# A value stage of graph attention: targets' places broadcast and compared with the lane, in place of one-hots turned on TensorE

## The chip, the core and the metric

The program runs on one core of a Trainium2 chip. Its engines work side by side and meet at semaphores: PE (TensorE: matmuls, and turning tiles by a matmul with the identity), DVE (VectorE), ACT (ScalarE), POOL (GpSimd) and SP, which here issues transfers. The metric is the device time of one execution in microseconds, the median of the runs. Time before: 7192.23 us (three runs, 7168.37 to 7201.24).

## The reference, cut to what matters

Four graph layers follow each other on one graph of 3125 nodes and 53125 edges (sorted by target). The change lies in the second, graph attention with eight heads of 32 features:

```python
def _mhsa(h, edge_bias, src, dst, Wq, Wk, Wv, Wp, bp):
    Q, K, V = h @ Wq, h @ Wk, h @ Wv                 # 3125 x 8 x 32
    score = einsum('ehd,ehd->eh', K[src], Q[dst]) / sqrt(HD) + edge_bias
    m = segment_max(score, dst)
    ex = exp(score - m[dst])
    denom = segment_sum(ex, dst)
    attn = ex / denom[dst]
    out = segment_sum(attn[:, :, None] * V[src], dst)
    return out.reshape(n, DIM) @ Wp + bp
```

The fourth layer needs for each edge one number more, the norm: 1 over the count of edges with the same target and the same of eight types. The kernel takes it from the table of nodes in the same place in which it takes `m[dst]`.

## The kernel before

Edges are sorted by target into 440 tiles of 128 edges; a tile belongs to one of 25 blocks of 128 nodes. Four tiles (U = 4) are a group, so there are 110 groups. Within its block an edge's target has a place from 0 to 127 (column `D_LOC` of `edge_d`). `g.lane` holds each partition's own number.

The score stage (`score_pass`, line 1669 on) computes the scores of all edges, per block and head an upper bound `m`, and the counts per type. Its SP queue stores the gathered V rows sorted by edge in `v_sorted`. Its DVE queue begins with tables, the last of them `type_hot` (L1857), on which PE waits before its loop.

The value stage (`value_pass`) runs over the 110 groups, one instruction stream for each engine; `unrolled(groups, stages)` writes it out, and each stage's number is its lead: at step k a stage with lead 3 works on group k + 3. A queue is in order, so what stands first in the list of stages waits first. Per group n:

- SP loads 512 KB of V rows into one of `VR` = 5 buffers, when `total` has freed it (L1963).
- ACT, `mask`: one-hots of the targets' places, edges on partitions, in four activations and one over 512 elements (L1976, L1981).
- PE, `turn_hot`: turns the four one-hots so that nodes lie on partitions (L2016). ACT, `copy_hot`: copies them from PSUM to bf16 (L1987).
- PE, `expand`: four small matmuls with the turned one-hots bring m and the inverse counts of each edge's target, in three bf16 parts (L2027).
- DVE: `join` adds the three parts (L2059), `lower` subtracts m from the scores (L2067) and takes the edge's own type (`mine`, L2070), `choose_norm` sums it into the norm (L2074).
- ACT, `exponents`: exp into the value buffer (L1993). POOL, `weigh`: values times exp (L2005).
- PE, `total`: four fp32 matmuls of 264 columns, each in two passes, into four banks (L2037). DVE, `add(0)` to `add(3)`: adds each bank to its block in `sums` (L2086); each add waits for the one before it. `starts_of` loads four registers from a table ahead of the first add and ahead of `expand`.

DVE prepares the table of parts first (L2046 to L2054) and zeroes the 6600 elements of `sums` (L2055).

The order by lead before: ACT `(3, copy_hot), (4, mask), (1, exponents)`; PE `(3, turn_hot), (2, expand), (0, total)`; DVE `(2, join), (2, lower), (0, add(0)), (2, choose_norm), (0, add(1)), (0, add(2)), (0, add(3))`.

Later passes (`fused_pass`, `last_pass`) wait on PE and ACT for values that `filled_for` (L162) and `end_of` (L175) load from tables into registers; they are paced by gathers that POOL issues.

Of the kernel before, what the change touches and what calls it, by code (L numbers as in the profile page):

```python
# [161 lines left out]
def filled_for(nc, g, plan, n):  # L162

    return nc.values_load_multi_w_load_instructions(
        plan.filled[0:1, bass.ds(n, 1)], engines=[PE], min_val=1, max_val=g.NB,
        skip_runtime_bounds_check_because="the sort has made them from the number of blocks")[1][0]
# [8 lines left out]
def end_of(nc, g, plan, k):  # L175

    return load_one(nc, ACTE, plan.ends, k, 1, g.NT // U + 1)
# [1486 lines left out]
def score_pass(core, g, acc, q_parts, kv_table, score, type_hot, digits, by_node):  # L1664
# [12 lines left out]
    with core.phase() as s:  # L1677
# [29 lines left out]
            s.sem(n) for n in ("cleared", "opened", "chosen", "typed", "picked", "dve_step"))  # L1707
        with core.nc.Block() as block:
            @block.sync
            def _(sp):  # L1710
                for n in range(groups):
                    q = n % KR
                    sp.wait_ge(gathered[q], (n // KR + 1) * (16 * U))
                    sp.dma_start(g.v_sorted[:, n * U:(n + 1) * U, :], kg[q][:, :, D:2 * D]).then_inc(stored[q], 16)
                for q in range(KR):
                    sp.wait_ge(stored[q], 16 * len(range(q, groups, KR)))

            @block.scalar
            def _(act):
                act.wait_ge(opened, 2)  # L1720
                act.activation(choose[:, :, :], turned_nodes, ACT.Copy).then_inc(picked, 1)

# [12 lines left out]
                def copy_hot(n):  # L1735
                    act.wait_ge(counted, n + 1)
                    if n >= HR:
                        act.wait_ge(turned, n - HR + 1)
# [41 lines left out]
            def _(pe):  # L1780
# [4 lines left out]
                step.then_inc(opened, 1)  # L1785
                pe.wait_ge(opened, 1)
# [142 lines left out]
def value_pass(core, g, acc, score, type_hot, ahead):  # L1929
# [4 lines left out]
    groups, NB, NT, VR = g.NT // U, g.NB, g.NT, 5  # L1934
    edge_f = g.edge_d[:, :, :].bitcast(F32)
    E = H + R
    with core.phase() as s:
        val = [s.sb(f"val{q}", [P, U, D + H]) for q in range(VR)]
        far = s.sb("far", [P, U, P])
        hot = [s.sb(f"hot{q}", [P, U, P]) for q in range(VR)]  # L1940
        hotT = [s.sb(f"hotT{q}", [P, U, P], BF16) for q in range(2)]
        theirs = [s.sb(f"theirs{q}", [P, U, E]) for q in range(2)]
        less, mine = ([s.sb(f"{n}{q}", [P, U, H]) for q in range(2)] for n in ("less", "mine"))
# [3 lines left out]
        psT = s.ps("psT", [P, U, P])  # L1947
        psE = [s.ps(f"psE{r}", [P, U, PARTS, E]) for r in range(2)]
        psA = [s.ps(f"psA{u}", [P, BANK]) for u in range(U)]
        loaded = [s.sem(f"loaded{q}") for q in range(VR)]  # L1950
        measured, hotted, turned, copied, spread, joined, lowered, picked, normed, expd, weighed = (
            s.sem(n) for n in ("measured", "hotted", "turned", "copied", "spread", "joined", "lowered", "picked", "normed",
                               "expd", "weighed"))
        summed, added = ([s.sem(f"{n}{u}") for u in range(U)] for n in ("summed", "added"))
        cleared, dve_step, ahead_in = s.sem("cleared"), s.sem("dve_step"), s.sem("ahead_in")
        with core.nc.Block() as block:
            @block.sync
            def _(sp):
                for n in range(groups):
                    q = n % VR  # L1960
                    if n >= VR:
                        sp.wait_ge(summed[U - 1], n - VR + 1)
                    sp.dma_start(val[q][:, :, 0:D], g.v_sorted[:, n * U:(n + 1) * U, :]).then_inc(loaded[q], 16)  # L1963
                    if n == VR:
                        for to, ap in ahead:
                            sp.dma_start(to, ap).then_inc(ahead_in, 16)
                sp.wait_ge(ahead_in, 16 * len(ahead))

            @block.scalar
            def _(act):  # L1970
                def mask(n):
# [7 lines left out]
                    if n >= VR:  # L1979
                        act.wait_ge(summed[U - 1], n - VR + 1)  # L1980
                    act.activation(hot[n % VR][:, :, :], far[:, :, :], ACT.Relu, scale=-1.0, bias=1.0).then_inc(hotted, 1)  # L1981

                def copy_hot(n):
                    act.wait_ge(turned, n + 1)
                    if n >= 2:
                        act.wait_ge(spread, n - 1)
                    act.activation(hotT[n % 2][:, :, :], psT[:, :, :], ACT.Copy).then_inc(copied, 1)  # L1987

                def exponents(n):
                    act.wait_ge(lowered, n + 1)  # L1990
                    if n >= VR:
                        act.wait_ge(summed[U - 1], n - VR + 1)
                    act.activation(val[n % VR][:, :, D:D + H], less[n % 2][:, :, :], ACT.Exp).then_inc(expd, 1)  # L1993

                act.preload_act_table_set("natural_log_exp_and_others")
                unrolled(groups, [(3, copy_hot), (4, mask), (1, exponents)])

            @block.gpsimd
            def _(pool):
                def weigh(n):  # L2000
                    q = n % VR
                    pool.wait_ge(loaded[q], n // VR * 16 + 16)
                    pool.wait_ge(expd, n + 1)
                    v = val[q][:, :, 0:D].rearrange("p u (h d) -> p u h d", h=H)
                    pool.tensor_tensor(v, v, bc(val[q][:, :, D:D + H], 3, HD), ALU.mult).then_inc(weighed, 1)  # L2005

                unrolled(groups, [(0, weigh)])

            @block.tensor
            def _(pe):  # L2010
                def turn_hot(n):
                    pe.wait_ge(hotted, n + 1)
                    if n:
                        pe.wait_ge(copied, n)
                    for u in range(U):
                        step = pe.transpose(psT[:, u, :], hot[n % VR][:, u, :], g.ident[:, :])  # L2016
                    step.then_inc(turned, 1)

                def expand(n):
# [3 lines left out]
                    pe.wait_ge(copied, n + 1)  # L2023
                    if n >= 2:
                        pe.wait_ge(joined, n - 1)
                    for u in range(U):
                        step = pe.matmul(psE[n % 2][:, u, :, :].rearrange("p k e -> p (k e)"), hotT[n % 2][:, u, :],  # L2027
# [4 lines left out]
                def total(n):  # L2032
                    pe.wait_ge(weighed, n + 1)
                    for u in range(U):
                        if n:
                            pe.wait_ge(added[u], n)
                        pe.matmul(psA[u][:, 0:D + H], hot[n % VR][:, u, :], val[n % VR][:, u, :], start=True, stop=True)\  # L2037
                            .then_inc(summed[u], 1)

                unrolled(groups, [(3, turn_hot), (2, expand), (0, total)])  # L2040

            @block.vector
            def _(dve):
# [11 lines left out]
                link(dve.memset(acc[:, :, 0:TOP], 0.0))  # L2055

                def join(n):
                    dve.wait_ge(spread, n + 1)
                    dve.tensor_reduce(theirs[n % 2][:, :, :], psE[n % 2][:, :, :, :].rearrange("p u k e -> p u e k"), X, ALU.add)\  # L2059
                        .then_inc(joined, 1)  # L2060

                def lower(n):
                    c = slice(n * U, (n + 1) * U)
                    dve.wait_ge(joined, n + 1)
                    if n >= 2:
                        dve.wait_ge(expd, n - 1)
                    dve.tensor_tensor(less[n % 2][:, :, :], score[:, c, :], theirs[n % 2][:, :, 0:H], ALU.subtract).then_inc(lowered, 1)  # L2067
                    if n >= 2:
                        dve.wait_ge(normed, n - 1)
                    dve.tensor_tensor(mine[n % 2][:, :, :], theirs[n % 2][:, :, H:E], type_hot[:, c, :], ALU.mult).then_inc(picked, 1)  # L2070

                def choose_norm(n):
# [290 lines left out]
```

## Time and profile before

| what | before |
|---|---|
| median of three runs | 7192.23 us (7168.37 to 7201.24) |
| span of the profiled execution | 6546.8 us |
| busy in the span: PE, DVE, ACT, POOL | 65%, 48%, 30%, 68% |
| value stage, 2800 to 3160 us of the span: PE, DVE, ACT, POOL busy | 273, 247, 252, 191 of 360 us |
| in it: granted TensorE clock, share of the DMA engines, moved | 1.00, 0.49, 148 GB/s |

The profile shows one execution. A row of the timeline gives the start in the span, the duration, engine, line and operation, what it writes and reads, and in square brackets the time in which the engine sat idle before it and what ended that. Durations of operations that follow each other on an engine overlap a little, so that distances between starts say what an engine needs. The span is shorter than the device time; the rest lies before and behind it.

### The profile page before, as it was taken

The page shows a single profiled execution, that of the slowest core. Times are in us where ns is not written, and L with a number is a line of the kernel's source. Part 1 is how long each engine was busy: PE and PEld are TensorE (multiplying, and loading weights), DVE is VectorE, ACT ScalarE, POOL GpSimd, SP SyncE. Part 2 cuts the span into 40 slices and gives each one's busy share as a digit, 9 for nine tenths or more (in the row PEclk, how much of TensorE's full clock was granted, in tenths as well). Part 3 has the DMA queues.
Part 4 walks back from the last instruction along what each step waited for, and adds up shares of the span by engine and source line. Part 5 has one row for each costly group of instructions (what it writes and reads, how often), then busy time and mean ns, then how long its engine had stood idle before and what let it go on. Part 6 is the DMA issues. An engine that isn't in the chain of part 4 may idle for free. (4 is left out here: it accounts for less than half of the span.)

```text
span 6546.8 us, 76038 instructions
## 1 busy us (share of the span) xinstructions
PE 4238.7 (65%) x20428; PEld 2969.8 (45%) x20491; DVE 3153.8 (48%) x6738; ACT 1977.5 (30%) x4507; POOL 4457.0 (68%) x4303
## 2 busy tenths in 40 slices
PE   2100888888776666577797555455577868876555
PEld 1000566666544555366595333333344435553433
DVE  5050455555568888866645322232244434444443
ACT  3720566666435555367373000000000000000000
POOL 2777777777668888455421777677677757776776
PEclk6555899999889888799998767777678989897777
DMA  3111222222146666444202555555556644444334
GB/s 92 54 45 53 73 74 75 75 75 74 24 154 212 208 210 212 136 141 148 71 1 68 162 162 163 151 162 162 147 183 201 205 132 148 154 148 106 106 106 93
DMA packets 450925, 812.27 MB, mean 124 GB/s; under 512 B 144458, under 2 KB 300221, under 8 KB 444096
## 3 DMA queue, kind: packets, MB, share of 16 engines
q0 software_dynamic: 209808, 566.12, 30.9%
q1 hardware_dynamic: 240816, 242.44, 11.5%
q8 instruction: 151, 2.47, 0.2%
q14 instruction: 150, 1.23, 0.1%
HBM read 650.48 MB, written 157.79 MB: 123 GB/s over the span
## 5 line engine op out<-in xcount | busy, mean ns | idle before, releaser
L1349 POOL DMA_INDIRECT p_rows<-table,idx_s x1320 | 1285.9, 974 | 572.8 <-issue 376.8
L1394 PE MATMUL p_psA<-p_rows,p_hot 128*128 128x256 bf16 (+1 forms) x4840 | 935.5, 360 | 727.3 <-DMA p_rows<-table,idx_s 546.7
L1394 PEld LDWEIGHTS p_psA<-p_rows,p_hot 128*128 128x128 bf16 (+1 forms) x4840 | 640.1, 138 | 997.5 <-issue 846.9
L571 POOL DMA_INDIRECT rec_s<-p_rec_out,p_row_s x416 | 428.4, 1030 | 231.7 <-issue 125.9
L585 POOL DMA_INDIRECT p_space<-h_table,p_space x440 | 475.3, 1080 | 134.1 <-issue 134.1
L1349 POOL DMA_INDIRECT p_rows<-rel_table,edge_d x440 | 429.1, 975 | 181.2 <-issue 128.3
L1557 POOL DMA_INDIRECT p_rows<-rel_table,edge_d x440 | 440.4, 1001 | 162.0 <-issue 130.4
L655 PE MATMUL p_psW<-p_wf,p_upto 128*128 128x256 f32 x1760 | 462.8, 422 | 115.7 <-DVE p_upto L815 114.8
L1423 ACT ACTIVATE sums<-p_psA,inv_degree 128x256 f32<-128x256 f32 x75 | 35.6, 474 | 1638.8 <-PE p_psA L1394 1638.8
L1903 DVE TENSOR_REDUCE sums<-p_psM 128x8 f32<-128x1024 f32 x440 | 518.3, 1217 | 4.3 <-PE p_psM L1829 3.8
L1766 POOL DMA_INDIRECT p_kg<-kv_table,edge_d x440 | 424.2, 964 | 141.1 <-issue 110.5
L376 POOL DMA_INDIRECT rec_d<-edge_d,norm x416 | 410.7, 987 | 159.2 <-issue 125.9
L1572 PE MATMUL p_psA<-p_rows,p_hot 128*128 128x256 f32 x880 | 333.6, 545 | 251.3 <-DMA p_rows<-rel_table,edge_d 221.1
L655 PEld LDWEIGHTS p_psW<-p_wf,p_upto 128*128 128x128 f32 x1760 | 365.5, 212 | 257.5 <-ACT p_psW L724 172.9
L1829 PE MATMUL p_psM<-p_splitT,p_choose 128*128 128x256 bf16 x1760 | 310.8, 307 | 264.0 <-DVE sums L1903 261.2
L1572 PEld LDWEIGHTS p_psA<-p_rows,p_hot 128*128 128x128 f32 x880 | 229.5, 273 | 355.6 <-issue 312.5
L823 DVE SCALAR_TENSOR_TENSOR p_space<-p_psW,p_space 128x256 f32<-128x256 f32 x440 | 182.5, 477 | 411.7 <-DMA p_space<-h_table,p_space 384.9
L2005 POOL TENSOR_TENSOR p_val<-p_val 128x1024 f32<-128x1024 f32 x110 | 210.3, 1912 | 241.6 <-ACT p_val L1993 241.6
L1449 DVE COPY p_xT<-p_psT 128x256 f32<-128x256 f32 x125 | 52.9, 423 | 628.8 <-PE p_psT L1367 628.7
L1829 PEld LDWEIGHTS p_psM<-p_splitT,p_choose 128*128 128x128 bf16 x1760 | 163.4, 106 | 334.1 <-DVE sums L1903 285.4
L1488 DVE COPY p_o<-p_psO 128x512 f32<-128x512 f32 x200 | 138.3, 692 | 348.7 <-PE p_psO L1381 348.7
L2037 PE MATMUL p_psA<-p_val,p_hot 128*128 128x264 f32 x880 | 227.9, 402 | 92.7 <-POOL p_val L2005 92.0
(352 smaller groups left out, 8760.7 us busy)
## 6 DMA issues: line engine op xcount, KB each, us to landing
v_sorted<-p_kg SPq DMA_DIRECT2D x110, 512.0 KB, 3.9
p_val<-v_sorted SPq DMA_DIRECT2D x110, 512.0 KB
rel_table<-p_o SPq DMA_DIRECT2D x50, 1024.0 KB
p_rows<-table,idx_s POOLq DMA_INDIRECT x1320
p_space<-rec_s SPq DMA_DIRECT2D x110, 136.0 KB, 2.1
p_rows<-rel_table,edge_d POOLq DMA_INDIRECT x880
p_rec_out<-edge_attr SPq DMA_DIRECT2D x103, 128.0 KB, 2.4
table<-p_o SPq DMA_DIRECT2D x50, 192.0 KB
```

Source lines behind the costliest of these rows:

```text
L376: pool.indirect_dma_start(g.rec_d_rows, bass.IndirectOffsetOnAxis(ap=g.row_d[:, j:j + 1], axis=0), g.rec_all[:, j, :], None).then_inc(sem, 16)
L571: pool.indirect_dma_start(g.rec_s_rows, bass.IndirectOffsetOnAxis(ap=row_s[:, n * U + u:n * U + u + 1], axis=0), rec_out[q][:, u, :], None ...
L585: pool.indirect_dma_start(msg[q][:, u, :], None, table, bass.IndirectOffsetOnAxis(ap=rec_i[q][:, u, S_IDX:S_IDX + 1], axis=0))\
L655: step = pe.matmul(psW[r][:, u, :], hid[t.q][:, k, (2 * r + u) * P:(2 * r + u + 1) * P], wf2[:, k, :], start=False, stop=(k == KT - 1), sk ...
L1349: pool.indirect_dma_start(rows[q][:, u, :], None, table, bass.IndirectOffsetOnAxis(ap=idx(n * U + u), axis=0))\
L1394: step = pe.matmul(psA[:, bass.ds(at[u], D)], hot[q][:, u, :], rows[q][:, u, c * D:(c + 1) * D], start=False, stop=(c == terms - 1), skip_ ...
L1557: pool.indirect_dma_start(rows[q][:, u, :], None, table, bass.IndirectOffsetOnAxis(ap=idx(n * U + u), axis=0))\
L1572: step = pe.matmul(psA[:, bass.ds(at[u], D)], hot[t.q][:, u, :], rows[t.q][:, u, :], start=False, stop=True, skip_group_check=True)
L1766: pool.indirect_dma_start(kg[q][:, u, :], None, kv_table, bass.IndirectOffsetOnAxis(ap=g.edge_d[:, j, D_SRC:D_SRC + 1], axis=0))\
L1829: last = pe.matmul(psM[k % 2][:, h, :], choose[:, k % 2 * (H // 2) + h, :], splitT[n % SR][:, tiles, :].rearrange("p u n -> p (u n)"), sta ...
L1903: dve.tensor_reduce(best[:, k % 2 * (H // 2):(k % 2 + 1) * (H // 2), at:at + half], psM[k % 2][:, :, :].rearrange("p h (u n) -> p h u n", ...
L2037: pe.matmul(psA[u][:, 0:D + H], hot[n % VR][:, u, :], val[n % VR][:, u, :], start=True, stop=True)\
```

## The change

The places of all edges (integers under 128, exact in bf16) are written once, in the score stage, to DRAM in order of edges: four turnings on PE, a copy on ACT and one transfer (`loc_rows`). In the value stage SP brings the 512 places of a group to all 128 partitions (`partition_broadcast`), and DVE compares them with the partition's own number (`show`): this gives the turned one-hots in bf16. `turn_hot`, `copy_hot` and their PSUM tile go. `join` and `lower` and the exponents work on two groups at once, `theirs` keeps all groups, and the norm is picked for ten groups at once (`pick`). `expand`, `join` and `lower` lead by five groups, `show` by six; there are eight value buffers, six banks for the totals, and the memset of `sums` is issued on POOL. The two registers that `filled_for` and `end_of` load are cut to eight bits by an `&`.

```diff
-        skip_runtime_bounds_check_because="...")[1][0]
+        skip_runtime_bounds_check_because="...")[1][0] & (2 * P - 1)
...
-    return load_one(nc, ACTE, plan.ends, k, 1, g.NT // U + 1)
+    return load_one(nc, ACTE, plan.ends, k, 1, g.NT // U + 1) & (2 * P - 1)
...
# score_pass: SP, ACT, PE
+                sp.wait_ge(noted, 1)
+                sp.dma_start(g.loc_rows.rearrange("(p c) -> p c", p=groups), by_tile[:, :, :].rearrange("p u n -> p (u n)"))\
+                    .then_inc(kept_places, 16)
...
+                act.wait_ge(placed, 1)
+                act.activation(by_tile[:, :, :], psQ[0:groups, :, :].rearrange("p u f -> p (u f)")
+                               .rearrange("p (u n) -> p u n", u=U), ACT.Copy).then_inc(noted, 1)
...
+                for u in range(U):
+                    step = pe.transpose(places[:, u * P:(u + 1) * P],
+                                        edge_f[:, :, D_LOC].rearrange("p (t u) -> p u t", u=U)[:, u, :], g.ident[:, :])
+                step.then_inc(placed, 1)
+                pe.wait_ge(noted, 1)
...
# value_pass
-    groups, NB, NT, VR = g.NT // U, g.NB, g.NT, 5
+    groups, NB, NT, VR, HR, TR, LR, AR = g.NT // U, g.NB, g.NT, 8, 5, 3, 4, 6
...
+    E, PAIR, CHUNK = H + R, 2 * U, 10 * U
...
+                def bring_places(n):
+                    if n >= LR:
+                        sp.wait_ge(shown, n - LR + 1)
+                    sp.dma_start(rows[n % LR][:, :, :].rearrange("p u n -> p (u n)"),
+                                 g.loc_rows[n * U * P:(n + 1) * U * P].partition_broadcast(P)).then_inc(shown_in[n % LR], 16)
...
+                unrolled(groups, [(3, bring_places), (0, bring_values)])
...
-                unrolled(groups, [(3, copy_hot), (4, mask), (1, exponents)])
+                unrolled(groups, [(5, exponents), (3, mask)])
...
+                pool.memset(acc[:, :, 0:TOP], 0.0).then_inc(blanked, 1)
...
-                unrolled(groups, [(3, turn_hot), (2, expand), (0, total)])
+                unrolled(groups, [(5, expand), (0, total)])
...
-                link(dve.memset(acc[:, :, 0:TOP], 0.0))
...
+                def show(n):
+                    dve.wait_ge(shown_in[n % LR], n // LR * 16 + 16)
+                    if n >= TR:
+                        dve.wait_ge(spread, n - TR + 1)
+                    dve.tensor_scalar(hotT[n % TR][:, :, :], rows[n % LR][:, :, :], g.lane[:, 0:1], None, ALU.is_equal)\
+                        .then_inc(shown, 1)
...
+                    if n % 2 == 0:
+                        return
+                    p = n // 2
                     dve.wait_ge(spread, n + 1)
...
+                    dve.tensor_reduce(theirs[:, p * PAIR:(p + 1) * PAIR, :], psE[p % 2][:, :, :, :].rearrange("p u k e -> p u e k"),
+                                      X, ALU.add).then_inc(joined, 1)
...
+                    dve.tensor_tensor(less[p % 2][:, :, :], score[:, c, :], theirs[:, c, 0:H], ALU.subtract).then_inc(lowered, 1)
...
+                def pick(n):
+                    if (n + 1) % (CHUNK // U):
+                        return
...
+                    dve.tensor_tensor(mine, mine, type_hot[:, c, :], ALU.mult).then_inc(picked, 1)
+                    dve.wait_ge(picked, 2 * k + 1)
+                    dve.tensor_reduce(g.norm[:, c], mine, X, ALU.add).then_inc(picked, 1)
...
-                unrolled(groups, [(2, join), (2, lower), (0, add(0)), (2, choose_norm), (0, add(1)), (0, add(2)), (0, add(3))])
+                unrolled(groups, [(6, show), (5, join), (0, add(0)), (5, lower), (0, add(1)), (0, add(2)), (0, add(3)), (0, pick)])
```

## Rows read from the trace of the kernel before

**Rows 1.** The page: the span.

```profile
span 6546.8 us, 76038 instructions
```

**Rows 2.** Timeline, value stage's ends: start, us, engine, line, operation, tiles, [idle before].

```profile
2771.44 20.63 SPq L1963 DMA_DIRECT2D p_val<-v_sorted  x6
...
2777.90 5.56 DVE L2055 MEMSET sums<- 128x6600 f32 x1 [1.44 <-issue]
...
2789.18 0.43 DVE L2086 TENSOR_TENSOR sums<-sums,p_psA 128x264 f32 x1 [1.29 <-PE p_psA L2037]
...
3180.95 0.43 DVE L2086 TENSOR_TENSOR sums<-sums,p_psA 128x264 f32 x1 [0.20 <-DVE sums L2086]
```

**Rows 3.** Waits from 2800 to 3160: who waited for whom, us in total, times, longest.

```profile
POOL p_val L2005 <- ACT p_val L1993: 168.8, 101, 2.1
```

**Rows 4.** Line 2005: duration ns least/median/most, first and last start, form.

```profile
L2005 POOL TENSOR_TENSOR p_val<-p_val x110: 1903/1912/1964, 2785.8 to 3173.8; 128x1024 f32<-128x1024 f32 x110
```

**Rows 5.** Timeline, one turn of POOL, PE and ACT.

```profile
2931.11 1.91 POOL L2005 TENSOR_TENSOR p_val<-p_val 128x1024 f32<-128x1024 f32 x1 [2.08 <-ACT p_val L1993]
...
2933.08 2.05 PE L2037 MATMUL p_psA<-p_val,p_hot 128*128 128x264 f32 x8 [1.04 <-POOL p_val L2005]
...
2935.60 0.60 ACT L1987 ACTIVATE p_hotT<-p_psT 128x512 bf16<-128x512 f32 x1 [1.45 <-PE p_psT L2016]
...
2936.26 2.05 PE L2037 MATMUL p_psA<-p_val,p_hot 128*128 128x264 f32 x8 [0.59 <-POOL p_val L2005]
...
2937.93 0.21 ACT L1993 ACTIVATE p_val<-p_less 128x32 f32<-128x32 f32 x1
...
2938.28 1.91 POOL L2005 TENSOR_TENSOR p_val<-p_val 128x1024 f32<-128x1024 f32 x1 [2.08 <-ACT p_val L1993]
```

**Rows 6.** Timeline, one group of DVE.

```profile
2936.16 0.35 DVE L2059 TENSOR_REDUCE p_theirs<-p_psE 128x64 f32<-128x192 f32 x1
...
2936.66 0.18 DVE L2070 TENSOR_TENSOR p_mine<-p_theirs,type_hot 128x32 f32<-128x32 f32 x1
2937.12 0.43 DVE L2086 TENSOR_TENSOR sums<-sums,p_psA 128x264 f32 x1 [0.28 <-PE p_psA L2037]
...
2937.75 0.43 DVE L2086 TENSOR_TENSOR sums<-sums,p_psA 128x264 f32 x1
...
2939.01 0.43 DVE L2086 TENSOR_TENSOR sums<-sums,p_psA 128x264 f32 x1 [0.20 <-DVE sums L2086]
...
2939.35 0.35 DVE L2059 TENSOR_REDUCE p_theirs<-p_psE 128x64 f32<-128x192 f32 x1
```

**Rows 7.** Line 2118: durations as in rows 4.

```profile
L2118 DVE TENSOR_SCALAR rel_first<-base,mix x8: 479/482/549, 3593.8 to 3893.0; 128x512 f32<-128x512 f32 x8
```

**Rows 8.** Lines 2067 and 1202, durations; then timeline of DVE and POOL behind the stage.

```profile
L2067 DVE TENSOR_TENSOR p_less<-score,p_theirs x110: 191/193/511, 2783.9 to 3173.1; 128x32 f32<-128x32 f32 x110
...
L1202 DVE TENSOR_TENSOR p_stage<-sums x25: 408/827/901, 3184.1 to 3235.5; 128x256 f32 x15, 128x256 f32<-128x256 f32 x10
...
3195.67 0.72 POOL L1047 TENSOR_TENSOR p_scaled<-p_scaled,p_row 128x256 f32<-128x256 f32 x1 [0.60 <-DVE p_scaled L1136]
3195.85 0.83 DVE L1202 TENSOR_TENSOR p_stage<-sums 128x256 f32<-128x256 f32 x1
...
3196.47 0.80 POOL L1049 TENSOR_TENSOR big<-p_scaled,p_row 128x256 f32<-128x256 f32 x1
```

**Rows 9.** Line 2161, a memset on POOL: durations as in rows 4.

```profile
L2161 POOL MEMSET by_node<- x1: 951/951/951, 1845.3 to 1845.3; 128x1024 bf16 x1
```

**Rows 10.** Timeline, the score stage's first table that PE waits for.

```profile
1886.45 3.83 DVE L1857 TENSOR_TENSOR type_hot<-edge_d,iota 128x3520 bf16<-128x3520 f32 x1
```

**Rows 11.** The page: GB/s in 40 slices of the span, 163.7 us each.

```profile
GB/s 92 54 45 53 73 74 75 75 75 74 24 154 212 208 210 212 136 141 148 71 1 68 162 162 163 151 162 162 147 183 201 205 132 148 154 148 106 106 106 93
```

**Rows 12.** Line 164, durations; the page's group of line 1394 (busy, mean, idle before).

```profile
L164 PEldq ALU_OP  x100: 32/32/36, 5978.4 to 6495.1; - x100
...
L1394 PE MATMUL p_psA<-p_rows,p_hot 128*128 128x256 bf16 (+1 forms) x4840 | 935.5, 360 | 727.3 <-DMA p_rows<-table,idx_s 546.7
```

More of the change, by code:

```diff
@@ L165, in filled_for @@
         plan.filled[0:1, bass.ds(n, 1)], engines=[PE], min_val=1, max_val=g.NB,
-        skip_runtime_bounds_check_because="the sort has made them from the number of blocks")[1][0]
+        skip_runtime_bounds_check_because="the sort has made them from the number of blocks")[1][0] & (2 * P - 1)
 def load_one(nc, engine, table, k, low, high):
@@ L1707, in score_pass @@
             s.sem(n) for n in ("cleared", "opened", "chosen", "typed", "picked", "dve_step"))
+        by_tile = hotT[HR - 1][0:groups]
+        placed, noted, kept_places = (s.sem(n) for n in ("placed", "noted", "kept_places"))
         with core.nc.Block() as block:
@@ L1929, in value_pass @@
 def value_pass(core, g, acc, score, type_hot, ahead):
-    groups, NB, NT, VR = g.NT // U, g.NB, g.NT, 5
+    groups, NB, NT, VR, HR, TR, LR, AR = g.NT // U, g.NB, g.NT, 8, 5, 3, 4, 6
     edge_f = g.edge_d[:, :, :].bitcast(F32)
-    E = H + R
+    E, PAIR, CHUNK = H + R, 2 * U, 10 * U
+    assert groups % 2 == 0 and VR % 2 == 0 and NT % CHUNK == 0
     with core.phase() as s:
-        val = [s.sb(f"val{q}", [P, U, D + H]) for q in range(VR)]
+        val = s.sb("val", [P, VR, U, D + H])
         far = s.sb("far", [P, U, P])
[L1940 to L1943, printed above, removed]
+        hot = [s.sb(f"hot{q}", [P, U, P]) for q in range(HR)]
+        rows = [s.sb(f"locs{q}", [P, U, P], BF16) for q in range(LR)]
+        hotT = [s.sb(f"hotT{q}", [P, U, P], BF16) for q in range(TR)]
+        theirs = s.sb("theirs", [P, NT, E])
+        less = [s.sb(f"less{q}", [P, PAIR, H]) for q in range(2)]
         parts = s.sb("parts", [P, NB, PARTS * E], BF16)
@@ L1978, in mask, with exponents @@
                     act.wait_ge(measured, n + 1)
-                    if n >= VR:
[L1980 to L1993, printed above, removed]
+                    if n >= HR:
+                        act.wait_ge(summed, (n - HR + 1) * U)
+                    act.activation(hot[n % HR][:, :, :], far[:, :, :], ACT.Relu, scale=-1.0, bias=1.0).then_inc(hotted, 1)
+                def exponents(n):
+                    if n % 2 == 0:
+                        return
+                    p, q = n // 2, (n - 1) % VR
+                    act.wait_ge(lowered, p + 1)
+                    if n >= VR:
+                        act.wait_ge(summed, (n - VR + 1) * U)
+                    act.activation(val[:, q:q + 2, :, D:D + H],
+                                   less[p % 2][:, :, :].rearrange("p (v u) h -> p v u h", u=U), ACT.Exp).then_inc(expd, 1)
                 act.preload_act_table_set("natural_log_exp_and_others")
-                unrolled(groups, [(3, copy_hot), (4, mask), (1, exponents)])
+                unrolled(groups, [(5, exponents), (3, mask)])
             @block.gpsimd
@@ L2010, in _ @@
             def _(pe):
[L2011 to L2017, printed above, removed]
                 def expand(n):
@@ L2062, in lower @@
                 def lower(n):
[L2063 to L2070, printed above, removed]
@@ L2072, in choose_norm @@
[L2072 to L2074 removed]
+                    if n % 2 == 0:
+                        return
+                    p = n // 2
+                    c = slice(p * PAIR, (p + 1) * PAIR)
+                    dve.wait_ge(joined, p + 1)
+                    if p >= 2:
+                        dve.wait_ge(expd, p - 1)
+                    dve.tensor_tensor(less[p % 2][:, :, :], score[:, c, :], theirs[:, c, 0:H], ALU.subtract).then_inc(lowered, 1)
```

71 lines of the change are left out of this document (42 added, 29 removed).

## Prediction

> **What bounds the kernel now.** I read the page first. Its span is 6546.8 us [rows 1] against a median of 7192.23 us for the runs, so some 645 us lie around the span; the change touches nothing there, I take them as fixed, and a microsecond saved in the span is one saved in the time. No engine is full over the whole span, so an average says nothing; the stage has to be found and read by itself. The view of a tile (p_val) places the value stage: the first transfer is issued at 2771.44, the first add into `sums` starts at 2789.18, the last one at 3180.95 and lasts 0.43 [rows 2]. That is 409.9 us, of which 17.7 are filling and 392.2 hold 110 groups: 3.57 us a group.
>
> Then the waits of its steady part. The longest is POOL's for the exponents, 168.8 us in 101 groups, 1.67 each [rows 3], with a weighing that takes 1.91 [rows 4]. So POOL isn't the bound: it waits for an answer that is late. The timeline shows whom for [rows 5]. The weighing that starts at 2931.11 ends at 2933.02; `total` starts at 2933.08 and holds PE for 2.05; only behind it, in PE's order, stands `turn_hot`, so ACT's copy of the turned one-hots starts at 2935.60. Behind the copy ACT has `mask`, and only then `exponents`, at 2937.93; the next weighing but one starts at 2938.28. This loop of POOL, PE and ACT takes 7.17 and carries two groups: 3.585 each, the whole period. Nothing in it is full; it is long because `total`, `turn_hot`, `copy_hot`, `mask` and `exponents` stand in line with a lead of one group for the exponents.
>
> **What is next.** The vector engine's own order of one group [rows 6]: from join to the start of the product `mine` 0.50, from there to the first add 0.46 (the registers of `starts_of` are loaded there), three distances of 0.63 between the adds, and 0.34 to the next join. The sum is 3.19, and in that group PE held it up hardly at all (0.28, within the 0.46 that the registers want anyway). So DVE stands 0.38 us a group behind the loop, 42 us in all, and what the change does to its list decides the rest.
>
> **The change, part by part.**
> *Loop.* `turn_hot` and `copy_hot` go, exponents lead by five groups instead of one, six banks stand in place of four, eight value buffers in place of five. The weighing of group n then needs a lowering done four to five groups before; the loop above has over 12 us for its 7.17. It no longer ends last. ACT is left with mask, 1.7 to 1.9 us (end of the copy at 2936.20 to 2937.93), and half an exponential: about 2.1. PE's two totals start 3.18 apart with 0.59 of waiting [rows 5]: 2.59 of work with the turning in it, less without. POOL has 1.91. All three are below DVE.
>
> *DVE, added.* `show`: one comparison of 128x512 two-byte elements with one scalar per partition. The trace has none like it. The nearest row is a tensor_scalar with 512 elements and such a scalar on four-byte data, 0.48 [rows 7]; the other end is the smallest operation of the stage, 0.19 [rows 8]. I take 0.48, the row of the same form; behind an operation the next one starts some 0.09 before its end (0.43 against 0.34 in the adds [rows 6]), so I count 0.39. What the Trainium skill says of it stands apart: "VectorE: DVE Perf Modes", section "The perf-mode tier table", gives tensor_scalar four elements a cycle on bf16 in SBUF against two on fp32. No row here shows it; with it I estimate the show at 0.35, and the period 0.06 shorter.
>
> *DVE, halved or taken out.* A pair now has one join of 384 elements. From 32 to 264 elements an operation grows from about 0.19 to 0.43, 1.04 ns each, so the join grows from 0.35 to 0.55; 0.46 of it hides the register loads, so join to first add is 0.48. One lowering a pair stands in the gap between first and second add, where the reduction of the norm stood: 0.66 in place of 0.63. `mine` and the norm go out of the group: each ten groups one product and one reduction of 320 elements, 0.95 together, 0.10 a group.
>
> *Sum.* Group with a join: show 0.39, join to add 0.48, then 0.66 and twice 0.63, and 0.34: 3.13. Group without: show to add 0.48 (the registers again), three times 0.63, 0.34: 2.71. Mean 2.92, with the norm 3.02.
>
> *The port.* Rows show that DVE and POOL exclude each other in some forms. `lower` takes 0.191 at least and up to 0.511 [rows 8]. In the next stage a product of DVE that reads two operands from SBUF takes 0.41 alone and 0.83 when it starts 0.18 behind an operation of POOL; it ends at 3196.68, 0.29 behind POOL's end at 3196.39, and POOL's next, of the same shape as the one of 0.72, takes 0.80 [rows 8]. So DVE waits for POOL's instruction to end, and then goes ahead of POOL's next. The adds read one operand from PSUM and last 0.43 in every row, beside POOL or not [rows 6]. Whether the show is of the forms that wait no row tells. The Trainium skill does: "SBUF — State Buffer", section "SBUF: two separate sides", says that one port pair is an exclusive lock between GpSimd and a DVE operation in a two-port mode or with two SBUF inputs, for the whole instruction. That rule speaks against this change; the rows just read agree with it for the product. I take the wait as real. Its size follows from the phase: call the start of `lower` 0. The exponential follows at 0.25, the first weighing of the pair at 0.65 and ends at 2.56, the second follows at once. The adds end DVE's group at 1.92; there the show of the group without a join wants in, waits until 2.56 and ends at 2.85 instead of 2.40: some 0.35 lost to the adds. The second weighing ends by 4.8; the next show comes at about 5.0, the next lowering at 6.1, both free. So 0.35 a pair, 0.18 a group; bounds are 0 and the rivals below. Period 3.20.
>
> *Beginning and end.* The memset of 5.56 leaves DVE [rows 2] for POOL, where a memset of 1024 elements takes 0.95 [rows 9]: some 5.5 for 6600, beside DVE's preparation of 5 us. If the two exclude each other, DVE starts late by what it has saved. Filling is then 10.5 to 17.7; I take 13. The last groups have no show or join: 2.5 less.
>
> *What is hidden.* In the score stage PE turns the places (four turnings; the eight passes of `total`, which are larger, take 2.05) and ACT copies them (512 elements, as the 0.60 of the copy [rows 5]), beside the 3.83 of `type_hot` [rows 10], on which PE waits anyway; their small transfer lies beside 110 groups. Cost 0, at most 2. SP gets 110 more transfers of 128 KB; the wait of each for an old show stands ahead of the value transfers in its queue, and both have several groups of lead. The stage moves 141 to 148 GB/s, with these at a period of 3.2 about 205, and the score stage has moved 212 [rows 11]. The `&` adds a register operation of 0.032 on PE per group [rows 12]; in those passes PE idles 727 us, mostly for gathers [rows 12]. Cost 0, at most 18 (550 times 0.032) if nothing covered it.
>
> **Sum.** 13 + 110 x 3.20 - 2.5 = 362.5 against 409.9: 47.4 us less. 7192.2 - 47.4 = 7145 us.
>
> **Rivals.**
> 1. *The show finds the port free or is short.* For: the phase above is nearly free of POOL already. Period 3.02 less 0.06: 2.96, filling 10.5: 334 us, time 7116.
> 2. *The show waits at a random phase.* A weighing holds 1.91 of each period; a random arrival waits 1.91 x 1.91 / (2 x 3.54) = 0.52. Period 3.54, stage 400, time 7182: no change that can be told. For it: ACT may deliver the exponents late, behind a mask of 1.9, which shifts POOL onto both shows. Against: ACT has 2.1 of work in a period of 3.2.
> 3. *Slower: POOL keeps the port from one weighing to the next.* The exponents now come for two groups at once, so two weighings stand in line without a gap. If the second goes ahead of a waiting show, the show waits from 1.92 until 4.5, 2.5 a pair: period 4.2, stage some 475, time 7257. It decides from a wait of 0.57 a group on, where the period is again 3.58. Against: in the rows DVE went first.
> 4. *It doesn't do what it says:* a loop that I have not seen (banks, transfers behind SP's wait) keeps the period at 3.58. Time about 7190.
>
> **How the numbers follow.** Forecast 0.53, rivals 0.12, 0.22, 0.08, 0.05. A measurement of this kernel tells a difference from none from about 0.5% on, 36 us. The forecast's gain of 47 is near it: a further 0.13 of period, easily lost in waits of semaphores, brings it there; I put 0.08 of its 0.53 within 0.5%. Faster: 0.45 + 0.12 = 0.57. Same: 0.08 + 0.22 + 0.05 = 0.35. Slower: 0.08. Range: low end from rival 1, less the 10 us by which the runs scatter, 7106; high end past rivals 2 and 4, 7200; rival 3 and a share of the tails are left out.
>
> **What would show it.** Right: the stage takes about 360 us; POOL's wait for ACT stays (DVE paces it), but comes once a pair; DVE is over 80% busy there; the show's shortest is 0.3 to 0.5, and every second one is longer by some 0.4, ending 0.3 behind a weighing; the adds stay at 0.43. PE waits for adds or for shows, not for POOL. Wrong: a show of 1 to 2 us (rival 3), PE waiting for p_hotT with DVE idle (rival 4), a weighing far over 1.91, or transfers that end last at POOL.

## The result

The changed kernel takes 7134.12 us (median of four runs, 7129.15 to 7138.89) against 7187.71 for the kernel before (7168.37 to 7201.24; one run more than in the table above, which gives 7192.23): a ratio of 0.9934, 95% interval 0.9918 to 0.9950. Repeated on another chip beside the kernel before it gave 7142.97 against 7188.25, 0.9936 (0.9917 to 0.9956). So 54 and 45 us less, 0.75% and 0.64%; forecast were 47 us and 7145.

The page of after, the span, the engines' shares and what DMA moved in 40 slices:

```profile
span 7130.8 us, 75257 instructions
...
PE 4317.0 (61%) x20054; PEld 2955.9 (41%) x20055; DVE 3165.0 (44%) x6539; ACT 1916.6 (27%) x4343; POOL 4465.6 (63%) x4304
...
GB/s 85 46 41 54 55 65 67 66 66 67 42 25 178 210 210 213 189 168 215 43 0 122 145 147 140 147 147 146 129 170 176 176 114 133 131 134 97 97 97 87
```

The span is longer than that of before [rows 1], though the kernel is faster. Both pages can't be compared as wholes: beside the kernel before with one harmless edit (first experiment) the span is 7256.0. The page of before comes from a faster chip: around the span of after lie 2 us of a run of 7132.51, so a span of 6546.8 can't belong to a run of 7168 us or more, and a chip used below runs the same kernel in 6534.34. What is faster there is the passes with gathers: in slices 23 to 28 that page moves 151 to 163 GB/s [rows 11], the page of after 140 to 147. The value stage doesn't have this difference, and it is compared below.

The timeline of after at the stage's two ends (start, duration, engine, line, operation, idle before):

```profile
3070.29 1.76 SPq L1980 DMA_DIRECT2D p_locs<-loc_rows  x4
3070.30 5.60 POOL L2031 MEMSET sums<- 128x6600 f32 x1 [47.59 <-POOLq L80]
3070.34 5.68 DVE L2066 TENSOR_SCALAR sums<-sums 128x200 f32<-128x200 f32 x1 [1.49 <-PEq L80]
...
3083.97 1.91 POOL L2029 TENSOR_TENSOR p_val<-p_val 128x1024 f32<-128x1024 f32 x1 [8.07 <-ACT p_val L2016]
...
3085.88 0.35 DVE L2080 TENSOR_SCALAR p_hotT<-p_locs,lane 128x512 bf16<-128x512 bf16 x1 [2.09 <-DMA p_locs<-loc_rows]
...
3087.64 1.74 DVE L2080 TENSOR_SCALAR p_hotT<-p_locs,lane 128x512 bf16<-128x512 bf16 x1 [0.69 <-DMA p_locs<-loc_rows]
...
3089.99 3.86 PE L2057 MATMUL p_psA<-p_val,p_hot 128*128 128x264 f32 x8
...
3091.69 0.41 DVE L2126 TENSOR_TENSOR sums<-sums,p_psA 128x264 f32 x1
...
3425.73 0.43 DVE L2126 TENSOR_TENSOR sums<-sums,p_psA 128x264 f32 x1 [0.20 <-DVE sums L2126]
3426.07 0.48 DVE L2107 TENSOR_TENSOR p_theirs<-p_theirs,type_hot 128x320 f32<-128x320 f32 x1
3426.59 0.48 DVE L2109 TENSOR_REDUCE norm<-p_theirs 128x40 f32<-128x320 f32 x1
```

The groups of after by line, from 3060 to 3430 (busy us, mean ns | idle before):

```profile
L2029 POOL TENSOR_TENSOR p_val<-p_val 128x1024 f32<-128x1024 f32 x110 | 210.7, 1937 | 129.4 <-ACT p_val L2016 128.6 <-DMA p_val<-v_sorted 0.8
L2126 DVE TENSOR_TENSOR sums<-sums,p_psA 128x264 f32 x440 | 187.5, 426 | 61.6 <-DVE sums L2126 34.9 <-PE p_psA L2057 23.3
L2080 DVE TENSOR_SCALAR p_hotT<-p_locs,lane 128x512 bf16<-128x512 bf16 x110 | 64.1, 584 | 3.8 <-DMA p_locs<-loc_rows 3.8
```

The stage takes 3427.07 - 3070.29 = 356.8 us against 409.9 [rows 2], 53.1 less. The medians differ by 53.6, with an interval of about 36 to 59 by the ratio's. The stage is made of 21.4 us to the first add (17.7 before), 334.5 from there to the end of the last one, 3.04 a group (3.57 before), and 0.9 for the last picking of the norm.

One pair of groups in the middle, DVE and POOL of after:

```profile
3232.57 0.35 DVE L2080 TENSOR_SCALAR p_hotT<-p_locs,lane 128x512 bf16<-128x512 bf16 x1
3232.83 0.55 DVE L2088 TENSOR_REDUCE p_theirs<-p_psE 128x128 f32<-128x384 f32 x1
...
3233.30 0.42 DVE L2126 TENSOR_TENSOR sums<-sums,p_psA 128x264 f32 x1
...
3233.64 0.22 DVE L2099 TENSOR_TENSOR p_less<-score,p_theirs 128x64 f32<-128x64 f32 x1
3233.88 0.26 ACT L2016 ACTIVATE p_val<-p_less 128x64 f32<-128x64 f32 x1 [1.86 <-DVE p_less L2099]
3233.92 0.43 DVE L2126 TENSOR_TENSOR sums<-sums,p_psA 128x264 f32 x1
...
3234.28 3.83 POOL L2029 TENSOR_TENSOR p_val<-p_val 128x1024 f32<-128x1024 f32 x2 [2.09 <-ACT p_val L2016]
...
3235.52 0.82 DVE L2080 TENSOR_SCALAR p_hotT<-p_locs,lane 128x512 bf16<-128x512 bf16 x1
...
3236.27 0.42 DVE L2126 TENSOR_TENSOR sums<-sums,p_psA 128x264 f32 x1
...
3238.49 0.35 DVE L2080 TENSOR_SCALAR p_hotT<-p_locs,lane 128x512 bf16<-128x512 bf16 x1
```

To be seen here: DVE's list is full from show to show, 5.92 us a pair. The free show takes 0.35. The other one arrives 1.24 behind the start of the first weighing and lasts until 3236.34, 0.15 behind that weighing's end at 3236.19. POOL waits 2.09 once a pair for the exponents, and those wait for DVE.

### The profile page after: what moved, and what is told of

Its sections match the earlier page's. It is cut to its first block and busy times, and to the rows that moved or that the text cites. A ratio compares the mean times of both kernels' runs of the same rounds, so it can differ in the third digit from the quotient of the medians.

```text
span 7130.8 us, 75257 instructions
## 1 busy us (share of the span) xinstructions
PE 4317.0 (61%) x20054; PEld 2955.9 (41%) x20055; DVE 3165.0 (44%) x6539; ACT 1916.6 (27%) x4343; POOL 4465.6 (63%) x4304
## 5 line engine op out<-in xcount | busy, mean ns | idle before, releaser
L1394 PE MATMUL p_psA<-p_rows,p_hot 128*128 128x256 bf16 (+1 forms) x4840 | 895.0, 349 | 602.1 <-DMA p_rows<-table,idx_s 401.7
L1394 PEld LDWEIGHTS p_psA<-p_rows,p_hot 128*128 128x128 bf16 (+1 forms) x4840 | 622.1, 134 | 856.2 <-issue 714.3
L585 POOL DMA_INDIRECT p_space<-h_table,p_space x440 | 451.6, 1026 | 289.5 <-issue 126.9
L655 PE MATMUL p_psW<-p_wf,p_upto 128*128 128x256 f32 x1760 | 480.1, 434 | 183.9 <-DVE p_upto L815 163.3
L376 POOL DMA_INDIRECT rec_d<-edge_d,norm x416 | 426.4, 1025 | 238.2 <-issue 125.3
L655 PEld LDWEIGHTS p_psW<-p_wf,p_upto 128*128 128x128 f32 x1760 | 386.0, 222 | 325.0 <-ACT p_psW L724 179.5
L1437 DVE TENSOR_TENSOR p_hot<-iota,loc_s 128x512 bf16<-128x512 f32 x330 | 219.3, 687 | 276.6 <-DMA p_locs<-loc_rows 211.8
L1381 PE MATMUL p_psO<-big,p_xT 128*128 128x512 f32 (+1 forms) x500 | 240.7, 634 | 141.9 <-DVE p_xT L1449 135.3
```

The costliest lines, as they stand in the source:

```text
L376: pool.indirect_dma_start(g.rec_d_rows, bass.IndirectOffsetOnAxis(ap=g.row_d[:, j:j + 1], axis=0), g.rec_all[:, j, :], None).then_inc(sem, 16)
L585: pool.indirect_dma_start(msg[q][:, u, :], None, table, bass.IndirectOffsetOnAxis(ap=rec_i[q][:, u, S_IDX:S_IDX + 1], axis=0))\
L655: step = pe.matmul(psW[r][:, u, :], hid[t.q][:, k, (2 * r + u) * P:(2 * r + u + 1) * P], wf2[:, k, :], start=False, stop=(k == KT - 1), sk ...
L1381: step = pe.matmul(out, xT[(m - 1) % TURNS][:, c, :], w[:, c, c0:c1], start=(c == 0 and not biased), stop=(c == KT - 1))
L1394: step = pe.matmul(psA[:, bass.ds(at[u], D)], hot[q][:, u, :], rows[q][:, u, c * D:(c + 1) * D], start=False, stop=(c == terms - 1), skip_ ...
```

## The experiments

The theory: the old stage was bound by a loop of POOL, PE and ACT, the new one by DVE's list and, within it, by the port that DVE and POOL exclude each other from. Rivals: the new buffers and leads are what counts; the longer shows have another cause; in the filling, transfers are late whatever is done. The runs were made on three chips, on which the kernel before takes 7245.67, 6534.34 and 7188.25 us, so times are only compared within a chip. The stage hardly differs between chips and is read from each trace: filling from DVE's first operation to the first add, period from there to the end of the last add, by 110.

**The edit of the registers alone.**

```diff
-        skip_runtime_bounds_check_because="...")[1][0]
+        skip_runtime_bounds_check_because="...")[1][0] & (2 * P - 1)
...
-    return load_one(nc, ACTE, plan.ends, k, 1, g.NT // U + 1)
+    return load_one(nc, ACTE, plan.ends, k, 1, g.NT // U + 1) & (2 * P - 1)
```

> The kernel before with one part of the change alone: the two registers that filled_for and end_of load are cut to eight bits. Theory (hidden work): PE and ACT wait for gathers in those passes, so 550 register operations of 0.032 us cost nothing: the time of before within 5 us, period of the value stage still 3.57 us a group. Rival: they stand in the path of PE: up to 18 us more. The run also gives a second profile of what is otherwise the kernel before.

Measured: 7246.91 against 7245.67, ratio 0.9999 (0.9984 to 1.0015). The first add starts at 3111.1, the last at 3504.1: 3.58 a group, as in [rows 2]. The register operations cost nothing that this comparison could tell, and its interval excludes the rival's 18 us. The edit stands in all further runs.

**The exponents ahead of the mask, in the kernel before.**

```diff
-                unrolled(groups, [(3, copy_hot), (4, mask), (1, exponents)])
+                unrolled(groups, [(3, copy_hot), (1, exponents), (4, mask)])
```

> The kernel before (with the eight-bit cut), and in ACT's list of the value stage the exponents stand ahead of the mask; nothing else. Theory: the stage is bound by the loop weighing, total, turning, copy, mask, exponents, 7.17 us for two groups; without the mask's 1.8 us in it the loop is 5.3, and DVE's own list of 3.19 a group bounds: 3.2 to 3.25 a group, 37 to 42 us less than before, some 7148. Rival (the long leads, the broadcast and the further buffers are what is needed): the period stays near 3.57 and the time near 7188.

Measured: 7214.52 against 7245.67, ratio 0.9947 (0.9928 to 0.9966), 31 us less; first add at 3113.7, last at 3475.8, 3.30 a group, where 3.2 to 3.25 and 37 to 42 us were expected. The durations of its `lower` (least, median, most):

```profile
L2067 DVE TENSOR_TENSOR p_less<-score,p_theirs x110: 191/652/1791, 3108.9 to 3467.9; 128x32 f32<-128x32 f32 x110
```

Its timeline, one turn of ACT and PE, with POOL and DVE:

```profile
3251.53 0.60 ACT L1987 ACTIVATE p_hotT<-p_psT 128x512 bf16<-128x512 f32 x1 [0.74 <-PE p_psT L2016]
...
3252.02 0.22 ACT L1993 ACTIVATE p_val<-p_less 128x32 f32<-128x32 f32 x1
3252.14 1.26 ACT L1976 ACTIVATE p_far<-iota,edge_d 128x128 f32<-128x128 f32 x4
...
3252.38 1.91 POOL L2005 TENSOR_TENSOR p_val<-p_val 128x1024 f32<-128x1024 f32 x1 [1.37 <-ACT p_val L1993]
...
3253.30 0.35 DVE L2059 TENSOR_REDUCE p_theirs<-p_psE 128x64 f32<-128x192 f32 x1
...
3253.43 0.63 ACT L1981 ACTIVATE p_hot<-p_far 128x512 f32<-128x512 f32 x1
...
3253.69 0.65 DVE L2067 TENSOR_TENSOR p_less<-score,p_theirs 128x32 f32<-128x32 f32 x1
...
3254.12 0.66 PE L2016 MATMUL p_psT<-ident,p_hot 128*128 128x128 f32 x4
...
3254.81 0.60 ACT L1987 ACTIVATE p_hotT<-p_psT 128x512 bf16<-128x512 f32 x1 [0.75 <-PE p_psT L2016]
```

The loop theory holds: one place in ACT's list gives over half of the change's gain, with no new buffer and no transfer. But what paces this kernel next is not DVE's list, as expected; it is a second, shorter loop of ACT and PE. ACT's copy at 3251.53 is followed without a gap by the exponents and by the mask, which ends at 3254.06; PE's turning starts at 3254.12 and ends at 3254.78, and the next copy starts at 3254.81: 3.28 for one group, the period in nearly every group. DVE doesn't set it. In a few places DVE falls behind by some 0.35, and then it needs 3.19 and 3.20 for the next two groups until it has caught up: its own list [rows 6] is 3.19. Else `lower`, with two operands from SBUF, meets a weighing and ends 0.05 behind it, here at 3254.34 behind POOL's 3254.29. The broadcast takes `turn_hot` and `copy_hot` out and with them this second loop; whether long leads alone would do as well was not tried.

**Without the weighing.**

```diff
-                    pool.tensor_tensor(v, v, bc(val[:, q, :, D:D + H], 3, HD), ALU.mult).then_inc(weighed, 1)
+                    pool.sem_inc(weighed, 1)
```

> The kernel after with the multiplication of the values by their exponentials left out (POOL only raises the semaphore), so POOL uses no port in the loop. Theory (DVE bounds, and every second show waits for POOL's port): all shows of the loop take 0.35 us, the pair of groups takes 5.66 us in place of 5.93, the period with the norm 2.92 in place of 3.04, 13 us less in the stage. Rival (the longer shows come from something else, their two waits or the transfers): every second show stays at 0.82 and the period at 3.04. Rival (weighing is in the path): the period falls below 2.8.

This kernel leaves the weighing out, so the values are summed unweighted; it serves for its times alone. Measured: 7168.76 in one run, without an interval; what counts is the trace. The durations of the show, here and in after:

```profile
L2080 DVE TENSOR_SCALAR p_hotT<-p_locs,lane x110: 344/347/355, 3107.0 to 3412.9; 128x512 bf16<-128x512 bf16 x110
```

The same row of after:

```profile
L2080 DVE TENSOR_SCALAR p_hotT<-p_locs,lane x110: 343/354/1744, 3080.7 to 3407.8; 128x512 bf16<-128x512 bf16 x110
```

With POOL idle no show of 110 is longer than 0.355. First add at 3116.9, last at 3430.4: 2.85 a group. The theory expected 2.92 and a pair of 5.66. DVE of this run: the pair takes 5.54 (3250.48 to 3256.02), and the add behind a free show stands 0.34 behind it, where the forecast had 0.48.

```profile
3250.48 0.35 DVE L2080 TENSOR_SCALAR p_hotT<-p_locs,lane 128x512 bf16<-128x512 bf16 x1
3250.82 0.43 DVE L2126 TENSOR_TENSOR sums<-sums,p_psA 128x264 f32 x1
...
3256.02 0.35 DVE L2080 TENSOR_SCALAR p_hotT<-p_locs,lane 128x512 bf16<-128x512 bf16 x1
```

The port costs 5.92 - 5.54 = 0.38 a pair, 21 us in all, and nothing else lengthens the shows. The weighing's own time isn't in the path: the period stays above 2.8, and DVE's list is as full as before.

**One comparison for two groups.**

```diff
-    groups, NB, NT, VR, HR, TR, LR, AR = g.NT // U, g.NB, g.NT, 8, 5, 3, 4, 6
+    groups, NB, NT, VR, HR, TR, LR, AR = g.NT // U, g.NB, g.NT, 8, 5, 4, 8, 6
...
-                    dve.tensor_scalar(hotT[n % TR][:, :, :], rows[n % LR][:, :, :], g.lane[:, 0:1], None, ALU.is_equal)\
-                        .then_inc(shown, 1)
+                    dve.tensor_scalar(hotT[:, n % TR:n % TR + 2, :, :], rows[:, n % LR:n % LR + 2, :, :], g.lane[:, 0:1], None,
+                                      ALU.is_equal).then_inc(shown, 1)
...
```

> The kernel after with one comparison of 1024 elements for two groups, at the place of the even show, when POOL has finished its pair of weighings; hotT has 4 and the places 8 buffers. Theory (port wait in the odd show): comparison 0.48 us and never lengthened, pair 5.65 in place of 5.93, period 2.92 with the norm, 13 us less, and 3 to 4 us less of filling, since the places of group 4 and later no longer wait for the first shows: 7118. Rival (no port wait, only DVE's count of instructions matters): the comparison is lengthened wherever it stands, and the gain is under 5 us.

Measured: 7173.98 against 7245.67, ratio 0.9889 (0.9849 to 0.9929). The comparison in this run:

```profile
L2083 DVE TENSOR_SCALAR p_hotT<-p_locs,lane x55: 477/480/2151, 3105.0 to 3411.3; 128x1024 bf16<-128x1024 bf16 x55
```

Its median is the free one; only two of 55, both in the filling, meet weighings. First add at 3112.8, last at 3432.2: 2.91 a group, filling 18.2, both as expected. By the trace that is 18 us less than after; the ratio's interval is too wide to confirm the size.

**Eight buffers of places**, `LR` 4 to 8, nothing else.

> The kernel after with eight buffers of places in place of four. In the profile of after, the first add of the value stage came 21.4 us behind its first transfer, and three of the first shows waited 3.8 us in all for places that SP could only ask for behind the first shows. Theory: these waits go and the filling is 18 to 19 us; the period stays at 3.04. Rival (the transfers, not their start, are late, since value transfers fill the queues): the shows wait as before and the filling stays at 21.

Measured: DVE's first operation at 2762.9, first add at 2782.7, last at 3116.0: filling 19.8, period 3.03. No show waits for a transfer any more, yet the filling is only 1.5 shorter, where 18 to 19 us, 2.4 to 3.4 less, were expected. The shows that come earlier meet weighings: the sixth and seventh take 2.01 and 1.99, in after 1.74 and 0.88. So the transfers were late because they were asked for late, as the theory has it, but part of the 3.8 us of waits comes back as waits for the port.

**The zeroing on ACT.**

```diff
-                pool.memset(acc[:, :, 0:TOP], 0.0).then_inc(blanked, 1)
...
+                act.activation(acc[:, :, 0:TOP], bc(bc(g.iota[:, 0:1], 1, NB)[:, :, 0], 2, TOP), ACT.Copy).then_inc(blanked, 1)
```

> The kernel after with the zeroing of the sums on ACT (a copy of a column of zeros) in place of POOL's memset. Theory (POOL's memset of 5.60 us holds the port, and DVE's first operation, 5.68 us in place of 0.27, waits for it): that operation is back at 0.27 and DVE is ready 5.4 us earlier; the filling falls from 21.4 to 16 or 17. Rival (the first places or values land no earlier anyway): the operation is short, but the first add comes at 20 us or later.

Measured: DVE's first operation, here and in after (durations, and where it stands):

```profile
L2066 DVE TENSOR_SCALAR sums<-sums x1: 268/268/268, 2764.8 to 2764.8; 128x200 f32<-128x200 f32 x1
```

The same row of after:

```profile
L2066 DVE TENSOR_SCALAR sums<-sums x1: 5680/5680/5680, 3070.3 to 3070.3; 128x200 f32<-128x200 f32 x1
```

First add at 2780.9: filling 16.1, 5.3 less than in after, as expected; period 3.03. POOL's memset had held up DVE for its whole length.

**Four banks for the totals**, `AR` 6 to 4, nothing else.

> The kernel after with four PSUM banks for the totals in place of six. Theory: PE (2.51 us a group) stands far enough ahead of DVE's adds only with more than four; with four a total waits for the add of one group before, and behind a late show PE's next expand and total are late too: period 3.1 to 3.3. Rival (DVE's list alone bounds): 3.04 with four as well, and the banks are worth nothing.

Measured: first add at 2790.3, last at 3124.4, period 3.04: my expectation was wrong, and the rival right. PE does wait for adds here (87.5 us of its weight loads, 3.7 in after), but the period doesn't show it: DVE still sets the pace, and the two banks more are worth nothing.

**Everything together, with join, show and lower between the adds.** The kernel also has the zeroing on ACT, the paired comparison with `TR` 6 and `LR` 10, and places that lead by five; the diff shows DVE's order.

```diff
-                unrolled(groups, [(6, show), (5, join), (0, add(0)), (5, lower), (0, add(1)), (0, add(2)), (0, add(3)), (0, pick)])
+                unrolled(groups, [(0, add(0)), (5, join), (0, add(1)), (8, show), (0, add(2)), (5, lower), (0, add(3)), (0, pick)])
```

> What the runs point to, together: one comparison for two groups, zeroing on ACT, ten buffers of places and six of turned one-hots, and DVE's list reordered so that join, show and lower of a pair stand between the adds of its even group, where DVE otherwise idles 0.29 us at each: add, join, add, show, add, lower, add. Theory (adds 0.63 apart are the floor of 5.04 us a pair): pair of 5.4 to 5.5, period 2.8 with the norm, filling 14 to 17: the stage takes 320 to 325 us against 357 of after, some 1.1% to 1.2% below the kernel before. Rival (PE, 2.5 to 2.6 a group, or transfers at over 240 GB/s bound first, or the show meets the weighings at its new place and is lengthened): the period stays at 2.9 or more.

Measured: 6459.60 against 6534.34, ratio 0.9885 (0.9868 to 0.9901). Filling 13.2 (2762.3 to 2775.5), period 2.87 (last add at 3090.6), stage 329. DVE, from one pair to the next, and its product for the norm:

```profile
2950.28 0.55 DVE L2091 TENSOR_REDUCE p_theirs<-p_psE 128x128 f32<-128x384 f32 x1
...
2951.08 0.48 DVE L2083 TENSOR_SCALAR p_hotT<-p_locs,lane 128x1024 bf16<-128x1024 bf16 x1
...
2951.82 0.22 DVE L2102 TENSOR_TENSOR p_less<-score,p_theirs 128x64 f32<-128x64 f32 x1
...
2955.59 0.55 DVE L2091 TENSOR_REDUCE p_theirs<-p_psE 128x128 f32<-128x384 f32 x1
```

The durations of the product for the norm in this run:

```profile
L2110 DVE TENSOR_TENSOR p_theirs<-p_theirs,type_hot x11: 486/1636/1653, 2804.0 to 3090.9; 128x320 f32<-128x320 f32 x11
```

The pair is 5.31, shorter than the 5.4 to 5.5 expected. The period is longer than the 2.8 expected and the stage than the 320 to 325, since the norm's product, also with two operands from SBUF, now stands where POOL weighs.

**The norm picked when POOL is idle**, behind the show instead of behind the last add, all else as there.

```diff
-                unrolled(groups, [(0, add(0)), (5, join), (0, add(1)), (8, show), (0, add(2)), (5, lower), (0, add(3)), (0, pick)])
+                unrolled(groups, [(0, add(0)), (5, join), (0, add(1)), (8, show), (-1, pick), (0, add(2)), (5, lower), (0, add(3))])
```

> As the version with pair comparison, zeroing on ACT and join, show and lower between the adds, and the picking of the norm moved from the end of a pair, where its product met a weighing (1.27 and 1.64 us in place of 0.48 in the profile), to the place behind the show, when POOL is idle. Theory (port): the product is 0.48 each time, 11 times some 1 us less, period 2.77 in place of 2.87, 10 us less. Rival: the delay of lower behind it passes on to POOL and PE, and the period stays at 2.85 or more.

Measured, beside after on one chip: 7110.50 against 7188.25, ratio 0.9891 (0.9873 to 0.9909). The product is free in all 11 places:

```profile
L2110 DVE TENSOR_TENSOR p_theirs<-p_theirs,type_hot x11: 481/483/484, 3114.9 to 3390.0; 128x320 f32<-128x320 f32 x11
```

First add at 3084.5, last at 3389.7: 2.78 a group and 13.8 of filling, a stage of 320 us. Against after on the same chip it is 32 us less (by the stages 36); the ratios' intervals don't overlap. Against the version before it, the 10 us of this one move stand in the traces alone: the two ratios, 0.9885 and 0.9891 on two chips, don't tell the versions apart.

**After, again.**

> The changed kernel once more, on the chip of the run above, so that both stand against the kernel before on one chip. Both theories: a stage of 357 us, period 3.04, and some 53 us less than before in absolute time, whatever the chip's time for the passes with gathers is.

Measured: 7142.97 against 7188.25, 45 us less, where 53 were expected; the ratio's interval reaches from 32 to 60. Filling 21.1 (3080.5 to 3101.6), last add at 3435.6, period 3.04: the stage is that of the first trace.

## Why the prediction was right, and where it wasn't

- *What bounded before.* Right: the loop. Shown by the exchange of two entries in ACT's list, 31 us. What stood behind it in that kernel was wrong: not DVE's 3.19 but the loop of copy, mask and turning at 3.28. It did no harm, since the change takes the turning and the copy out.
- *What is next.* Right for the changed kernel: DVE's list. POOL waits for ACT (117.3 us from 3090 to 3410), ACT for DVE (108.1), PE for DVE's shows (55.6), and DVE is busy for 82% of 3100 to 3400. Without the port's waits, with one comparison for two, and with operations moved between the adds, the period fell each time.
- *The show.* 0.48 was taken from the row of four-byte elements; 0.35 is measured, and 0.48 for 1024 elements, so 0.26 ns an element where the adds want 1.04. The trace agrees with the Trainium skill ("VectorE: DVE Perf Modes", "The perf-mode tier table"), whose four elements a cycle had given 0.35. This term was 0.13 us a pair too large.
- *The registers* were counted behind a show without a join, 0.48; without a wait it is 0.34. 0.14 too large. The first gap of the adds was 0.04 too large. Together the list without the port was forecast at 5.84 a pair and is 5.54.
- *The port.* Forecast 0.35 a pair, measured 0.38. The show arrives 1.24 behind the first weighing's start (forecast 1.27) and takes 0.82, 0.47 more than alone, ending 0.15 behind the weighing (forecast 0.29). The phase was right: only the show of the group without a join meets POOL, and DVE goes ahead of POOL's second weighing. That is what rival 3 had wrong; rival 2 (random phase) fell with it, since the weighings start from `lower` and so keep their place. (By its own terms rival 3's period is 3.02 + 1.25 = 4.27, not 4.2.) The rule of the Trainium skill ("SBUF — State Buffer", "SBUF: two separate sides") holds for four forms here: the comparison, the subtraction, the product of the norm, and, against POOL's memset, a tensor_scalar.
- *Period*: 3.20 forecast, 3.04 measured, 17.5 us too much over 110 groups. These are sizes; the mechanism was as forecast.
- *The filling*: 13 forecast, 21.4 measured, outside the bounds of 10.5 to 17.7. The step that failed: I charged the filling with the memset alone and put the long leads at nothing. The memset cost what the upper bound gave it: DVE's first operation 5.41 longer, the first add 5.3 later; 2.5 of it were in the 13. Without it the filling is still 16.1, not 10.5. What the forecast lacks is seen in the trace of after: the first weighing ends at 3085.88, but PE starts its first total only at 3089.99, 4.1 later, since in its order the expansion of the sixth group stands ahead, and this waited for a show that started at 3087.64, behind late places, and took 1.74 beside a weighing. With the zeroing on ACT the same wait is 4.2. Eight buffers of places give back 1.5. Shorter leads weren't tried, and weren't needed: with the zeroing on ACT, ten buffers and one comparison for two groups the filling is 13.2 with leads no shorter, so they are dear only while the shows come late. The low end of 10.5 has no working either: 17.7 less the memset's 5.56 gives 12.1.
- *The end.* 2.5 was taken off for the last groups. In the measurement it lies within the mean of 3.04 and isn't told apart.
- Part of the hit is luck: the misses of the period, -17.5, and of the filling, +8.4, the 2.5 and the last picking of 0.9 offset each other to -5.7 us, so that the forecast of 362.5 for the stage met 356.8.
- *645 us around the span* was wrong, and so is the sentence above that the rest lies before and behind the span. Around the span of after there lie 2 us (7130.8 in a run of 7132.51); the page of before came from a faster chip. It did no harm because only a difference within the stage was carried over, and the stage takes 3.57 to 3.58 a group on both chips.
- *Hidden work.* Right for the registers (0.9999). Right for the work in the score stage: from DVE's first operation in it to the value stage's first transfer it takes 884.0 and 886.1 us in the first two experiments, without the places, and 886.6 and 884.7 in the next two, with them, on the same chip.

## What to carry to other kernels

Before buffers and leads are added, find the loop and ask which step in it waits only because of its place in a queue: one exchange took 31 us from the stage here, the whole change 53. Then look for the next loop before you credit the busiest engine with the bound: an engine whose operations are merely lengthened by a lock looks full. In a stage where DVE and POOL both work, sort DVE's operations by whether they need the shared port, and put those that do where POOL has nothing. The port's waits were 21 us here; with one comparison for two groups, the gaps between the adds used and a shorter filling it came to a further 32 us. Count the filling as a term of its own; long leads and a memset on POOL's side both lengthen it.

## What the runs showed of the hardware

- A memset of POOL, which reads nothing, holds up a one-operand tensor_scalar of DVE for its whole 5.6 us: 5.68 beside it, 0.27 with the zeroing on ACT.
- When a DVE operation waits for POOL's first of two back-to-back products, it goes between them: it ends 0.15 behind the first, and POOL's two take 3.83 in place of 3.79 (free in the run with the paired comparison).
- Chips differ: the same kernel took 6534, 7188 and 7246 us. Between the trace of before and that of the first experiment 600 of the 709 us lie in the five stretches in which POOL issues gathers or scatters; the value stage, fed by large transfers, takes 409.9 and 411.2.
